# A macaron block on one core: one list of steps for the run, other places for the splits, and reciprocals of the exps' sums computed by GpSimd

## What is computed

```python
x = L0_attn_x                                   # (8, 1024, 256), float32
x = x + 0.5 * ffn(layernorm(x))
x = x + attn(layernorm(x))
x = x + 0.5 * ffn(layernorm(x))

def ffn(x):       # 16 heads of 16 columns
    q, k, v = heads(x @ Wq), heads(x @ Wk), heads(x @ Wv)
    a = softmax(einsum('bqd,bkd->bkq', q, k) / sqrt(D), axis=-1)
    z = merge(einsum('bkq,bkv->bqv', a, v)) @ Wo
    z = l2_normalize(l2_normalize(z) @ Wff)
    return gelu(z)                              # exact gelu

def attn(x):      # 8 heads, no softmax: linear attention
    q, k, v = heads(x @ w_qkv.T + b_qkv)
    return merge(einsum('bhij,bhjd->bhid', einsum('bhid,bhjd->bhij', q, k), v)) @ w_o.T + b_o
```

## Time and profile before

| | us |
|---|---|
| median of three runs | 3015.58 (3014.48 to 3017.93) |
| the profiled run | 3017.08 |
| its span in the profile | 3015.3 |
| PE busy | 2731.6 (91%) |
| DVE busy | 2799.6 (93%) |
| ACT busy | 2721.6 (90%) |
| POOL busy | 901.7 (30%) |

### The profile page before, as it was taken

The page is one execution under the profiler, slowest core; times in us unless marked ns, Lnnn a source line. Parts: engine busy times, 40 slices in busy tenths (PEclk is TensorE's granted clock), DMA queues, the critical chain, the costliest instruction groups (busy, mean ns, idle before and its releaser), DMA issues.

```text
span 3015.3 us, 88294 instructions
## 1 busy us (share of the span) xinstructions
PE 2731.6 (91%) x36160; PEld 1100.9 (37%) x36160; DVE 2799.6 (93%) x5659; ACT 2721.6 (90%) x5028; POOL 901.7 (30%) x1195
## 2 busy tenths in 40 slices
PE   5989999999999999999999998989988888898987
PEld 2323343433434434344343433333333333333333
DVE  4999999999999999999999999999999899998996
ACT  2999898998999989999898989999998999999997
POOL 3332323323233232332323323222332223233232
PEclk8999999999999999999999999999999999999999
DMA  8222341233412334123341233433233343322332
GB/s 222 56 46 65 58 100 33 51 74 58 93 37 54 74 57 92 36 53 78 58 84 41 54 79 71 85 57 73 54 63 69 71 85 56 71 50 60 79 71 57
DMA packets 155254, 205.53 MB, mean 68 GB/s; under 512 B 34529, under 2 KB 88289, under 8 KB 154722
## 3 DMA queue, kind: packets, MB, share of 16 engines
q1 hardware_dynamic: 154594, 199.37, 31.8%
q0 software_dynamic: 256, 0.52, 0.1%
HBM read 46.66 MB, written 25.17 MB: 24 GB/s over the span
## 4 chain that ended last, share of the span: by engine, by line
DVE 32%; PE 30%; SPq 16%; issue 8%; ACT 7%; POOL 5%; DMA 2%; POOLq 0%; ACTq 0%; DVEq 0%
DVE exp_ring L657 27%; SPq L375 16%; PE ring L771 12%; PE ring L834 8%; PE o_acc L848 8%; ACT exp_ring L581 5%; PE ring L893 2%; DMA kq_stack<-kq_parts 1%; POOL kq_rest L362 1%; POOL kq_parts L366 1%; POOL kq_parts L360 1%; POOL kq_parts L364 1%; DVE w_xn L727 1%; DVE x_post L682 1%; ACT w_xn L593 1%
## 5 line engine op out<-in xcount | busy, mean ns | idle before, releaser
L657 DVE TENSOR_SCALAR_CACHE_REDUCE exp_ring<-ring 128x1024 f32<-128x1024 f32 x2048 | 2404.2, 1214 | 134.2 <-PE ring L834 129.8
L581 ACT ACTIVATE exp_ring<-exp_ring,neg_max 128x1024 f32<-128x1024 f32 x2048 | 2338.2, 1144 | 189.4 <-DVE exp_ring L657 188.1
L834 PE MATMUL ring<-kq_stack 128*32 128x512 bf16 x16384 | 1168.1, 384 | 131.7 <-DVE exp_ring L657 84.9
L848 PE MATMUL o_acc<-exp_ring,v_scaled 128*32 128x512 f32 x8224 | 1088.2, 604 | 86.2 <-POOL v_scaled L514 62.3
L834 PEld LDWEIGHTS ring<-kq_stack 128*32 128x32 bf16 x16384 | 413.3, 97 | 1045.8 <-DVE exp_ring L657 470.5
L514 POOL TENSOR_TENSOR v_scaled<-v_now,exp_rsums 128x64 f32<-128x64 f32 x513 | 152.4, 298 | 1763.0 <-DVE exp_rsums L672 1749.2
L581 ACT ACTIVATION_READ_ACCUMULATOR exp_ring<-exp_ring,neg_max 128x1 f32 x2048 | 385.1, 188 | 0.0
L848 PEld LDWEIGHTS o_acc<-exp_ring,v_scaled 128*32 128x32 f32 x8224 | 254.0, 111 | 311.1 <-POOL v_scaled L514 85.1
L771 PE MATMUL ring<-ffn_wo_wowff,o_T 128*32 128x256 f32 x4352 | 259.2, 380 | 7.8 <-DVE exp_ring L657 6.4
L771 PE MATMUL ring<-xn_T,ffn_wqkv 128*32 128x512 f32 x2112 | 261.8, 616 | 3.0 <-DVE exp_ring L657 1.9
L360 POOL TENSOR_TENSOR kq_parts<-kq_stage,zero 128x512 bf16<-128x512 f32 x130 | 142.6, 1097 | 176.9 <-DMA kq_stack<-kq_parts 101.6
(11 more groups left out here) (102 smaller groups left out, 1302.1 us busy)
## 6 DMA issues: line engine op xcount, KB each, us to landing
kq_stack<-kq_parts SPq DMA_DIRECT2D x2072, 64.0 KB, 2.4
x_post<-x_slots SPq DMA_DIRECT2D x17, 1024.0 KB, 5.7
x_prep<-x_slots SPq DMA_DIRECT2D x16, 1024.0 KB, 8.4
x_slots<-x_post SPq DMA_DIRECT2D x8, 1024.0 KB, 5.4
out<-x_post SPq DMA_DIRECT2D x8, 1024.0 KB, 4.7
x_prep<-in_L_attn_x SPq DMA_DIRECT2D x1, 1024.0 KB, 5.6
exp_ring<-in_L_attn_w_qkv SPq DMA_DIRECT2D x1, 512.0 KB
kq_stack<-kq_parts POOLq DMA_DIRECT2D x8, 64.0 KB, 3.6
```

What stands on the lines that cost most here:

```text
L581: nc.scalar.activation(e, e, ACT.Exp, bias=negmax[:, i % NM:i % NM + 1], scale=-1.0, accum_out=sums[:, g % EG, c:c + 1]).then_inc(exp_done, 1)
L657: nc.vector.tensor_scalar(E[:, (g % EG) * HQ + c, :].rearrange("p (b n) -> p b n", b=NB), ps, -1.0, None, ALU.mult, ALU.min, accum_out=neg ...
L834: last = mm(ps[k:k + COLS, n, :], kq[:, 0, c, j * P + k:j * P + k + COLS], kq[:, 1, c, n * BANK:(n + 1) * BANK], start=True, stop=True)
L848: last = mm(O[32 * c:32 * c + 32, n, :], vsc[a][:, g % EG, c, :], E[:, (g % EG) * HQ + c, n * BANK:(n + 1) * BANK], start=(a == 0 and j == ...
```

## The change

It does these things.

- **One list.** section_steps and the bodies are replaced by one list for the run, which order(engine) sorts. A step knows its phase (kind, p, i), its rank on an engine and its PSUM slot, so that waits are computed step by step. Post steps of no phase and the preparation of phase 16 are no longer there. START, TAIL, PLAIN and LINEAR are the tables; SP's DMAs are steps in them too.
- **Places.** All places are new. GpSimd's splits come 2.5 tiles behind PE's qk (LEAD qk -2.5).
- **Reciprocals.** DVE's step recip is gone. GpSimd raises the four sums to the power of -1 (constant tile minus_one, instruction L515) and then scales v as before (L522), at the table's place + 1.5.
- **Parts.** On PE a step of several parts can be spread: gram into four parts half a tile apart, G into two a tile apart. av has its halves as steps of their own. x1 runs in four pieces.
- **Start.** x comes in two halves, PE's first transposes wait for each xn alone, weights are four steps among the others, and the three later of the four first splits (FIRST_SPLITS) run on ACT (copies to bf16) and DVE (differences). Of the 32 DMAs of the first stack GpSimd issues 18 instead of 8. Loads of x for phases 0 to 7 read the input directly; x_slots is only written by linear phases. The zeroing of exp_ring and the 8 matmuls on it are gone.
- **End.** The last phase's norms, gelus and stores run in two halves.

```diff
-    PLAIN = {
-        "recip": 5.1, "av": 9.1, "av_next": 2, "z": 7.7,
...
-        "x1": (72.1, 72.2),
...
-        "qk": (73.3, 85.4, 93.6, 101.4, 9.2, 21.2, 37.3, 41.7),
...
-    WITH_LINEAR = {
-        "recip": 5.1, "av": 8.1, "av_next": 2, "z": 6.1,
...
-        "gram": (52.4, 58.3),
+        "PLAIN": {
+            "recip": 3.5,
+            "av": 9.5,
+            "av_next": 1.5,
...
+            "x1": (70.1, 73.2, 73.7, 74.5),
...
+            "qk": (75.8, 83.8, 92.2, 100.1, 14.7, 19.9, 33.8, 37.7),
...
+        "LINEAR": {
+            "recip": 5.3,
+            "av": 8.2,
+            "av_next": 2,
...
+            "gram": (52.3, 58.3),
...
+    GAP = {'gram': 0.5, 'G': 1.0}
...
+            "pool": {"xn2": -1.5, "u_norm": -2.5, "qk": -2.5, "recip": -1.5, "xbias": -1.0, "xn": -2.5, "w_norm": -0.5, "x1": 1.0}}
...
-                    elif kind == "recip":
-
-                        dve.wait_ge(exp_done, START + p * TILES + HQ * r)
-                        nc.vector.reciprocal(rsum[:, i % EG, :], sums[:, i % EG, :]).then_inc(rsum_ready, 1)
...
+                elif kind == "recip":
+                    q, j = i // QG, i % QG
+                    half, a = q // 2, q % 2
+                    pool.wait_ge(exp_done, nth("act", "tile", p, HQ * i + HQ - 1))
+                    nc.gpsimd.tensor_tensor(rsum[:, i % EG, :], sums[:, i % EG, :], minus_one[:],
+                                            ALU.pow).then_inc(rsum_ready, 1)
+                    pool.wait_ge(rsum_ready, nth("pool", "recip", p, i))
...
+                elif (kind, p, i) in FIRST_SPLITS:
+                    n = FIRST_SPLITS.index((kind, p, i)) + 1
+                    hi, mid, lo = pieces(i // 2, i % 2)
+                    nc.scalar.activation(hi, ps[:, 0, :], ACT.Copy, scale=qk_scale(i)).then_inc(first_hi, 1)
+                    act.wait_ge(first_rest, n)
+                    nc.scalar.activation(mid, resid[:, 1, :], ACT.Copy, scale=1.0).then_inc(first_mid, 1)
...
+                    dve.wait_ge(first_hi, n)
+                    if n > 1:
+                        dve.wait_ge(first_lo, n - 1)
+                    nc.vector.scalar_tensor_tensor(out=resid[:, 1, :], in0=ps[:, 0, :], scalar=qk_scale(i), in1=hi,
+                                                   op0=ALU.mult, op1=ALU.subtract).then_inc(first_rest, 1)
+                    dve.wait_ge(first_mid, n)
+                    nc.vector.tensor_tensor(lo, resid[:, 1, :], mid, ALU.subtract).then_inc(first_lo, 1)
...
+                elif kind == "gram":
+                    pe.wait_ge(xn2_ready, (p + 1) * NT)
+                    for t in range(2 * part, 2 * part + 2):
+                        last = mm(ps[:, 0, i * P:D + 1], wb[:, t, i * P:(i + 1) * P], wb[:, t, i * P:],
+                                  start=(t == 0), stop=(t == NT - 1))
```

1183 lines of the change are left out of this document (601 added, 582 removed).

## The result

The changed kernel takes 2950.74 us (median of 4 runs, 2948.21 to 2952.47), the kernel before 3016.44 (4 runs on the same chip): a ratio of 0.9782, 95% interval 0.9765 to 0.9799. It is faster, inside the range of 2860 to 2957, but 45 us above the forecast of 2906 and outside the likeliest band of 2880 to 2935; the prediction had given 23% to the band where it fell.

The account below looks back on a forecast made before the run. DVE, PE and ACT were all read as close to full (93, 91, 90%), none alone explaining the span. Terms -12.5 - 12.5 - 39 - 32 - 9 - 5 = -110 us took 3015.58 to 2906 us; range 2860 to 2957, some 83%.

Parts of the forecast that it names:

- Part 1: Reciprocals moved from DVE to GpSimd as powers: 0.93 us each, 2.9 us a phase off DVE, no latency loss counted.
- The slower rival: Late v_scaled at each of 512 groups makes the kernel slower than before, up to 3264 us; chance 4%.
- Part 2: GpSimd's splits moved later in plain phases so none waits for a stack: -4.0 us of DVE's idle a phase.
- Part 3: Other orders, linear-attention phases: with the reciprocals' share, -4.9 us a phase, 8 times, -39 us.
- the gram's cut: Linear phases: cutting PE's run of 16 gram matmuls, after which DVE stands 2.18 us, saves 2.0 us a phase.
- The scattered idle time: Linear phases: a fifth of DVE's other 6.4 us of thinly spread idle time won by new places, -1.3 us.
- the port: Rival: powers hold up DVE's SBUF-to-SBUF instructions as splits do, 48 us in 16 phases, 2953 us; 23% together with moved waits.
- Part 4: Removed work: post steps in phase 0, -12.5 us; preparation of a phase 16 in phase 15, -9 us.
- Part 5: The ends: start -12.5 us by DMA issues (-7.4) and first splits and transposes (-5); drain -5 us by halves.
- the waits only move: Rival: v_scaled stay late behind splits, PE bounds linear phases; 2954 us; 23% together with the port rival.
- Everything in place: Rival: linear phases at 181 us and plain ones at 167.2, 2856 us in all; chance 13%.
- moved splits change nothing: Rival: moved splits and reciprocals have no effect; ends and removed work alone give 2977 us; chance 4%.

Follow-up runs that it names:

- e5: Changed kernel without any reciprocal: v is multiplied by the sums themselves, so the result is no softmax; 2933.3 us, ratio 0.973.
- e4: Changed kernel with a second, unused power per group on GpSimd in front of each v_scaled; 3057.5 us, ratio 1.014.
- e2: Kernel before with powers on GpSimd in place of VectorE's reciprocals, all places kept; 3062.0 us, ratio 1.015.
- e6: Changed kernel with reciprocals back on VectorE at place 5.1 in every phase, as in the kernel before; 2972.6 us, ratio 0.986.
- e8: Changed kernel with two splits' places in plain phases (73.3 and 9.2) and their leads as in the kernel before; 3041.6 us, ratio 1.009.
- e12: Changed kernel with gram in one piece in linear phases and GpSimd issuing 8 first-stack DMAs instead of 18; 2947.4 us, ratio 0.977.
- e7: Changed kernel with GpSimd issuing 8 first-stack DMAs and the last phase's norms and gelus in one piece; 2948.3 us, ratio 0.978.

## Where the prediction was right and where it failed

**Part 1, the powers: size right, cover nearly right.** 1.01 us for 0.93; "I count no loss" is 0.9 us a linear phase and 0.7 a plain one (e5), 17 us in the run. The slower rival, a late v_scaled at all 512 groups, is refuted at one power and would have come true at two: e4 is 1.4% slower than the kernel before.

**Part 2 and the reciprocals in plain phases: the sum right, the terms wrong.** The forecast was -5.3 a phase, made of -4.0 for the splits, -1.9 for the reciprocals and +0.6; measured -5.6. But the terms aren't additive, and the 1.98 us was read in one of the short phases, of 174.2 us, while the phases that gained most are the long ones. The reciprocals' move alone costs 4.4 us (e2), with the new places it brings 3.6 (e6), as it also frees VectorE from waits for exps. The splits' move is worth 12.6 us once powers stand on GpSimd (e8), though only 1.98 us of idle VectorE could be read at one of the two places. That no split waits for a stack in plain phases came true in phases 9 to 14; in phase 0 one waited 2.9 us.

**Part 3, linear phases: this step failed.** Of -4.9 us a phase, +0.4 was measured. Term by term: the gram's cut, -2.0 forecast, gives 0 within what the phases differ by (e12). VectorE's 2.18 us of the earlier trace rows were taken for a loss that can be cut away; the row ahead of it shows PE at work for 3.72 us, and by its busy time PE is idle only 1.5 us of 101.7 up to the end of the phase. What VectorE waits while PE does work that has to be done anyway is not won by dividing that work. That doesn't make PE the only bound: its busy time holds modelled ends, and in the same stretch its weight loads waited for VectorE at 22 tiles (891.4 to 993.08 us):

```profile
PEld ring L834 <- DVE exp_ring L657: 7.8, 22, 0.7
```

The reciprocals, -1.9 forecast: taking them off VectorE and putting nothing on GpSimd gives -1.0 (e6 against e5), and the powers give 0.9 back. That leaves -0.1. The scattered idle time, -1.3 forecast, and the 0.3 for powers beside VectorE's work together: +0.5, which is e6 against the kernel before (189.9 and 189.45), and no more than the phases differ by. No run prices the 0.3 alone; the rows on the port below give it no support. The prediction had written that VectorE's work "bring[s] nothing where PE is the bound" and still counted two thirds of it.

**Part 4.** Phase 0: -13.0 for -12.5. Phase 15: -6.6 for -9, up to the last z. Its tiles are done 10.6 us sooner, but ScalarE isn't: the last exps end 2.8 us behind VectorE's last tile, and then come a power and a slow av step. The tail of the changed kernel:

```profile
2919.51 0.19 ACT L568 ACTIVATION_READ_ACCUMULATOR exp_ring<-exp_ring,neg_max 128x1 f32 x1
2919.77 1.01 POOL L515 TENSOR_TENSOR exp_rsums<-exp_sums,minus_one 128x4 f32<-128x4 f32 x1 [3.15 <-ACT exp_ring L568]
2920.85 0.29 POOL L522 TENSOR_TENSOR v_scaled<-v_now,exp_rsums 128x64 f32<-128x64 f32 x1
...
2921.20 3.56 PE L811 MATMUL o_acc<-exp_ring,v_scaled 128*32 128x512 f32 x16 [2.60 <-POOL v_scaled L522]
...
2924.84 1.22 DVE L648 COPY o_T<-o_acc 128x1024 f32<-128x1024 f32 x1 [7.92 <-PE o_acc L811]
```

Nothing covers the power here, so it costs its full 1.01 us, once.

**Part 5.** Start -10.3 for -12.5, with the parts wrong: the issues of the stack's DMAs brought nothing (-7.4 forecast, from 0.74 us an issue taken as a fixed price; with 14 on SyncE it was 1.27), and what lies ahead of them brought 10.5 (39.78 to 29.29 us; 5 had been estimated). Of this 3.3 come from SyncE's first DMA starting at 0.75 us instead of 4.03: SyncE no longer raises the counters of COUNT_FROM_START ahead of it, which the prediction had not counted. The other 7 are left for the splits as turns of ScalarE and VectorE and the rest of the preparation; no run takes them apart. That the sum came near is luck. Drain -4.9 for -5; 2.9 of it by the halves (e7), the rest was not tested.

**The rivals.** Two rivals lie within 4 us of the result, *the port* (2953) and *the waits only move* (2954), and neither is what happened: their totals are right by chance. The second has the better picture of linear phases, where the gain is lost to PE and to a late v_scaled (PE waited 2.8 us for v_scaled in a linear phase before, 8.1 after). Its reasoning did not hold for plain phases, where moved splits and reciprocals gave 33 us. *The port* is refuted. VectorE's operations from SBUF to SBUF did not grow at the median: xn at 407 ns (406 before), xn2 at 404 (404 before); the means grew by 29 and 30 ns, 192 x 0.03 = 6 us of busy time in the run at most. Both lines, ns minimum, median, maximum:

```profile
L688 DVE TENSOR_SCALAR x_prep<-x_prep,bn_mv,rstd x128: 397/407/1342, 10.6 to 2655.1; 128x256 f32<-128x256 f32 x128
```

```profile
L702 DVE TENSOR_SCALAR w_xn<-x_post,bn_mv,rstd x64: 397/404/1323, 286.0 to 1624.6; 128x256 f32<-128x256 f32 x64
```

The long ones exist before and after. What they meet tells more: in the changed kernel 30 of the 128 operations of L688 run beside a power and neither a split nor another step of GpSimd, 402 ns at the mean and 410 at most, as against 402 and 412 for the 36 with GpSimd idle. The 16 of L702 beside a power took 413 ns (434 at most), eight pieces of x1 beside a power and its v_scaled 678. The powers themselves took 1.16 us at most. All that are long in these lines and in x1's stand beside a split. The rule of the Trainium skill, page "SBUF — State Buffer", section "Terms", has the one that comes second wait for the whole instruction of the other; for powers on 128x4 this trace doesn't agree as far as VectorE goes, for splits it does. *Everything in place* (2856) and *moved splits change nothing* (2977) fell.

The best version that was run, e12 (2947.4 us, ratio 0.977), can't be told from the changed kernel (0.978) by its interval.

## What to carry to other kernels

Idle time of an engine is a doubtful reserve if the engine it waits for is at work at that moment: read both over the same stretch before counting any of it. When a short operation moves to an engine with a queue, its own length is the small number; what it does behind a queue that stands, or in front of an engine that runs late, is the large one (-3.6 or +4.4 us a phase for the same move). And two edits that both touch one queue are to be priced together: the powers' sign in plain phases was set by the places of the splits. A mean over stages that are meant to be alike can hide two kinds; list them before taking a row from one.

## What the runs showed of the hardware

- DMA issue: SyncE took 1.27 us for each of 14 issues beside 18 of GpSimd, and 0.69 for each of 24 beside 8. SyncE's share of the 32 transfers of the first stack (64 KB each) took it 16.6 to 18.4 us, whether it was 14 or 24 of them.
- TensorE's clock: PE had been busy 29.7 of 35 us at a granted clock of 1.00, stood 1.66 us and then 2.60 us at the end of the last phase with 16 matmuls in 1.92 us between, and ran its next 16 matmuls at a granted clock of 0.53, near the lower of its two levels (1.2 of 2.4 GHz): 3.56 us. The same 16 had taken 1.92 us in the kernel before, at 1.00, behind a stand of 1.60 us.

```profile
2921.20:2924.76 3.56, 3.56 (x16) 0.60 (x16) 0.00 (x0) 0.00 (x0) 0.00 (x0) 0.53 0.00 0
```

```profile
2983.07:2984.99 1.92, 1.92 (x16) 0.42 (x16) 0.00 (x0) 0.00 (x0) 0.00 (x0) 1.00 0.00 0
```

- A power on GpSimd grew with its columns: 1.01 us on 128x4, 1.64 on 128x8, where a multiplication took 0.20 on 128x8 and 0.29 on 128x64.
- VectorE's operations with SBUF on both sides grew beside GpSimd's splits of 128x512, and more so when cut: x1 as two operations took 4.09 us beside one split, as four 6.01.
